# The place of three kinds of ScalarE copies, and of one product half, in a selective-scan kernel

## The reference, cut to what matters

```
xc    = causal 4-tap convolution of (in_proj_w @ ctx)      per channel
u     = silu(xc + conv_b)
B, C, dt = x_proj_w @ u                                     16, 16 and 32 rows
delta = softplus(dt_proj_w @ dt + dt_proj_b)
state = state * exp(delta * A) + (delta * u) * B            over 1024 positions, for 16 indices n
y     = (sum over n of state * C + D * u) * silu(layernorm(x) transposed)
x     = x + y transposed
xn    = layernorm(x)
out   = x + xn @ W_base.T + b_base + (two of eight rank-8 experts, gated by a softmax of the top two logits)
```

## Time and profile before

| | us |
|---|---|
| median of three runs | 2049.84 (2047.81 to 2057.35) |
| the profiled execution's own time | 2057.73 |
| its span, first to last instruction | 2055.7 |
| DVE busy | 1789.9 |
| POOL busy | 1729.5 |
| PE busy | 1767.3 |
| ACT busy | 1260.2 |
| mean granted TensorE clock | 0.916 of full speed |

### The profile page before, as it was taken

How to read it: one execution, slowest core, us unless ns; L and a number is a source line. 1 busy time by engine, 2 the same in 40 slices (tenths; PEclk the granted TensorE clock), 3 DMA queues, 4 the chain that set the end, 5 groups by cost and what they waited for, 6 DMA issues and landing times.

```text
span 2055.7 us, 23677 instructions
## 1 busy us (share of the span) xinstructions
PE 1767.3 (86%) x7996; PEld 1083.9 (53%) x7996; DVE 1789.9 (87%) x1435; ACT 1260.2 (61%) x1704; POOL 1729.5 (84%) x772
## 2 busy tenths in 40 slices
PE   9777777777788889898998889898888888888999
PEld 4344444454455555555555555555555555554554
DVE  3699999999999999999999999998999999996111
ACT  3466666656666676666666776666666676673331
POOL 0399999999999989899999999999999999996200
PEclk9887787777789999999999999999999999999999
DMA  4658665687766666688766666687676666666200
GB/s 157 243 190 290 202 205 194 194 297 269 229 214 201 222 205 216 214 301 279 244 207 220 222 212 211 224 283 260 225 223 214 203 213 216 220 205 217 80 31 31
DMA packets 158984, 435.87 MB, mean 212 GB/s; under 512 B 14640, under 2 KB 47664, under 8 KB 158864
## 3 DMA queue, kind: packets, MB, share of 16 engines
q1 hardware_dynamic: 155408, 421.78, 60.3%
q0 software_dynamic: 3456, 12.58, 3.1%
HBM read 383.46 MB, written 50.86 MB: 211 GB/s over the span
## 4 chain that ended last, share of the span: by engine, by line
DVE 40%; PE 31%; issue 19%; ACT 4%; POOL 3%; DMA 1%; DVEq 0%; SPq 0%; POOLq 0%; ACTq 0%
DVE state L1123 21%; DVE row L1108 13%; PE bank_a L544 9%; PE y_ps L488 6%; DVE conv L1100 3%; PE bank_b L544 3%; PE row L566 2%; POOL prod L1264 2%; PE row L482 2%; PE bank_b L439 1%; ACT decay L840 1%; PE bank_a L555 1%; DVE yy L1130 1%; PE bank_b L448 1%; PE bank_b L458 1%
## 5 line engine op out<-in xcount | busy, mean ns | idle before, releaser
L1264 POOL TENSOR_TENSOR prod<-state,c_rows 128x1024 f32<-128x1024 f32 x512 | 1207.2, 2383 | 87.9 <-DVE state L1123 47.6
L1123 DVE TENSOR_TENSOR_SCAN state<-decay,row 128x1024 f32<-128x1024 f32 x334 | 763.2, 2285 | 8.1
L488 PEld LDWEIGHTS y_ps<-ident,prod 128*128 128x128 f32 x4096 | 512.9, 151 | 274.9 <-issue 189.8
L488 PE MATMUL y_ps<-ident,prod 128*128 128x128 f32 x4096 | 581.8, 291 | 31.8 <-POOL prod L1264 31.4
L1108 DVE TENSOR_TENSOR row<-du,row 128x1024 f32<-128x1024 f32 x334 | 404.3, 1211 | 36.6 <-PE row L482 36.2
L1257 POOL TENSOR_TENSOR drive_rows<-du,b_rows 128x1024 f32<-128x1024 f32 x178 | 424.3, 2384 | 5.5 <-DMA b_rows<-bc_d 5.5
L544 PE MATMUL bank_a<-w_o,xnT 128*128 128x512 f32 x816 | 395.2, 615 | 19.6 <-DVE x L1170 19.6
L840 ACT ACTIVATE row<-delta,a 128x1024 f32<-128x1024 f32 x178 | 199.0, 1118 | 346.7 <-DVE state L1123 346.1
L1123 DVE TENSOR_TENSOR_SCAN state<-row,drive_rows 128x1024 f32<-128x1024 f32 x178 | 405.0, 2275 | 5.5 <-POOL drive_rows L1257 4.8
L840 ACT ACTIVATE decay<-delta,a 128x1024 f32<-128x1024 f32 x334 | 374.2, 1135 | 0.1
L482 PE MATMUL row<-parts,sel 96*128 96x512 bf16 x668 | 223.7, 420 | 157.3 <-DVE state L1123 151.1
(11 more groups left out here) (138 smaller groups left out, 1595.3 us busy)
## 6 DMA issues: line engine op xcount, KB each, us to landing
c_rows<-bc_d SPq DMA_DIRECT2D x512, 512.0 KB, 4.5
xrow<-in_x SPq DMA_DIRECT2D x32, 512.0 KB, 5.1
skip<-u_d SPq DMA_DIRECT2D x32, 512.0 KB, 9.0
yy_d<-yy SPq DMA_DIRECT2D x32, 512.0 KB, 6.5
b_rows<-bc_d SPq DMA_DIRECT2D x24, 512.0 KB, 9.4
u_d<-conv SPq DMA_DIRECT2D x24, 512.0 KB, 5.4
ctx<-u_d SPq DMA_DIRECT2D x48, 256.0 KB, 6.6
x<-in_x SPq DMA_DIRECT2D x24, 512.0 KB, 5.6
```

What stands on the lines that cost most here:

```text
L488: last = nc.tensor.matmul(y_ps[:, i * P:(i + 1) * P], source[:, i * P:(i + 1) * P], ident[:, :], start=(first and i % (H // P) == 0), stop ...
L1123: nc.vector.tensor_tensor_scan(state[:, q % STATES, :], factor, term, 0.0, ALU.mult, ALU.add).then_inc(scan_done, 1)
L1264: nc.gpsimd.tensor_tensor(prod[:, q % PRODS, :], state[:, q % STATES, :], c_rows[:, q % RING, :], ALU.mult).then_inc(prod_ready, 1)
```

## The change

On ScalarE, outside the last blocks, `take_v` in sections 1 and 2 and `take_gate` in sections 3 and 4 go from behind the section's decays to ahead of them. `take_turned`, of sections 3 and 4, stays where it is, so it is now behind `take_gate` and behind the decays. In section 11 `take_gates` goes ahead of `gate_rows`, behind the same table load. On TensorE, in the last blocks that are dense (15 and 23), the first product half stands in sections 8, 9, 10 and 11 in place of 6, 7, 9 and 10.

```diff
@@ tensor, section @@
                 if dense:
-                    if m in (6, 7, 9, 10):
-                        k = 2 * (6, 7, 9, 10).index(m)
+                    at = (8, 9, 10, 11) if last else (6, 7, 9, 10)
+                    if m in at:
+                        k = 2 * at.index(m)
                         product(j, 0, [k, k + 1], beside, True)
@@ scalar, section @@
+                last = r == NE - 1 and b + 1 < B
+                if not last and m in (1, 2) and E + 1 < NBLK:
+                    take_v(E + 1, m - 1)
+                if not last and m in (3, 4):
+                    take_gate(E, m - 3)
 
                 if (E, m + 1) in P_INDEX:
                     make_decay(E, m + 1)
...
-                last = r == NE - 1 and b + 1 < B
-                if not last and m in (1, 2) and E + 1 < NBLK:
-                    take_v(E + 1, m - 1)
...
                 if dense and m in (3, 4):
                     take_turned(j, m - 3, beside, True)
-                if not last and m in (3, 4):
-                    take_gate(E, m - 3)
...
                     if m == 11:
                         table(SILU)
-                        gate_rows(E + 1)
                 if dense and m == 11:
                     take_gates(j, beside)
+                if E + 1 < NBLK and m == 11:
+                    gate_rows(E + 1)
```

## The result

| | before | after |
|---|---|---|
| median, us (same chip) | 2053.6 (2047.81 to 2061.97) | 2086.22 (2082.67 to 2090.64) |
| ratio to before, 95% interval | | 1.0157 [1.0112, 1.0201] |
| span of the profiled execution | 2055.7 | 2088.6 |
| mean granted TensorE clock | 0.916 | 0.908 |

The change makes the kernel 32.6 us slower (23 to 41 by the interval). The forecast was 2059, the range 2038 to 2070: wrong, the time lies above the range. The direction and the mechanism were named; the size was over three times as large (+32.6 for +9.5). A small part is the start: the forecast was added to a median of 2049.8, and the median of this table is 2053.6.

The account below looks back on a forecast made before the run. VectorE was taken to set the pace, GpSimd just behind, with VectorE's waits mostly for TensorE. The terms +12 + 4 - 4 - 2.5 = +9.5 us on a median of 2049.8 gave 2059.3 us, range 2038 to 2070.

Parts of the forecast that it names:

- The order on ScalarE: Sections 3 and 4: ScalarE passes no waiting instruction, so xn's second turning starts 1.06 us later, 3.4 us after scan 2.
- The formula: Section 7's `spread` ends 10.14 us after the second turning starts, plus half the low-clock stretch behind that start.
- +12 for the projecting blocks: Sections 2 to 7, blocks 9 to 13 and 16 to 21: later second turning and low stretches cost +12 us (-1 to +24).
- D: Rival: nearly all blocks fall to the low clock, and late; two thirds of +24, in sum +18, 2068 us; chance 0.13.
- +4 for 14, 22 and 24 to 31: Blocks without projections, section 5: spare time shrinks from 1.63 to 0.57 us; low stretches cost +4 us (0 to 11).
- -4 for section 15: Sections 11 to 15, blocks without projections: turned gates copied 1.15 us earlier; half of 7.9 us waits goes, -4 (0 to -8).
- -2.5 for block 23, 0 for block 15: Moved product half and earlier gates' copy shorten VectorE's waits; GpSimd limits gains to -2.5 us (block 23), 0 (block 15).
- The non-dense blocks at 0: Blocks 0 to 8: they turn no xn, so the gate's copy delays nothing TensorE waits for; 0 us (-1 to 1).
- Rivals A to C: A: clock stays full, 2038, chance 0.22; B: low stretches keep places, 2048, 0.10; C: GpSimd absorbs gains, 2050, 0.05.
- A: Rival, sections 2 and 3: TensorE's 2.5 us idle is cut in pieces, clock stays full; -11.5 us, 2038; chance 0.22.

Follow-up runs that it names:

- gate_only: The kernel before with only `take_gate` moved ahead of its section's decays: 2079.63 us, ratio 1.0110 to before.
- after_turned_first: The changed kernel with `take_turned` put between `take_gate` and the decay: 2059.18 us, ratio 1.0021 to before.
- after_filled: The changed kernel with TensorE repeating transposes in idle time (first xn turning 4 times, gate's second turning twice): 2059.91 us, ratio 1.0028 to before.
- swapped_mid_filled: swapped_gates with the gates' transpose issued 8 times, the spread for section 12 twice, for section 13 three times: 2039.65 us, ratio 0.9931 to before.
- turned_swap: The kernel before with `take_turned` ahead of the decays and TensorE's second xn turning ahead of the gate's second: 2063.07 us, ratio 1.0034 to before.
- swapped_gates: The changed kernel, but `take_gate` where it was, `take_turned` ahead of the decay, xn's second turning ahead of the gate's: 2045.8 us, ratio 0.9963 to before.

## Why the prediction was wrong, point by point

**The order on ScalarE: right.** The second turning was put at 3.4 us after scan 2 and is at 3.38 in all 21 blocks that turn both; the 2.51 us wait is gone. ScalarE passes nothing that waits, as the Trainium skill ("PSUM — Partial Sum Buffer", section "Engine vs sequencer instructions") says. The trace agrees: in block 11 gate_only moves the turning from 2.35 to 3.38 us, and after_turned_first moves it back to 2.35, each by just the decay.

**The formula: right.** In block 12 the second turning starts 3.38 after scan 2 and the low stretch ends at 9.18: 3.38 + 10.14 + (9.18 - 3.38)/2 = 16.42; `spread` of section 7 ends at 788.40, 16.39 after. It comes out within 0.1 us in all eleven projecting blocks, before and after. What was wrong is what was put into it.

**+12 for the projecting blocks: this step failed.** Their waits in sections 5 and 7 rose from 7.9 to 30.8 us and the blocks from 643.5 to 665.0 us: +21.5. (The 7.6 us of the prediction left out 0.35 us in section 5 of block 20.) Its terms were a low stretch that ends at 6.3 on average, in eight blocks, and a chance of 0.4 in 11, 16 and 19. Ten of eleven fell; nine of them for 6.8 us, and the ends lie at 7.0 to 9.3, 8.6 on average. The average of 4.8 was carried 1.5 us later, as if the stretch were a thing that idle time carries with it. But the idle time now lies in three pieces (2.29, 1.20, 0.86 us) in front of work that used to run through, and the clock fell there in blocks that had never shown it. after_filled shows that this idle time matters: filled with repeats, it leaves no low stretch longer than 3.4 us there from block 10 on. The prediction had this case, D, at 13%, with +24, and priced it at two thirds.

**+4 for 14, 22 and 24 to 31: too small.** Section 5 costs 8.5 us (1.3 before) and section 8 2.8 (0): +10. A low stretch on the way was priced at 1.1 us, in four blocks of ten. It came in 22 and 25 to 31: in 22, 25 and 31, where it is 6.8 us long, section 5 waits 2.0 us, in the others 0.4 to 0.5. VectorE, after, block 25:

```profile
1549.43 1.23 DVE L1110 TENSOR_TENSOR row<-du,row 128x1024 f32<-128x1024 f32 x1 [2.00 <-PE row L482]
```

**-4 for section 15: half of it.** In the blocks without projections 7.9 became 6.1 us. (In the projecting blocks, put at 0, 4.5 became 1.4.) The early copy takes 1.12 us off the wait for the gates in block 25, and the idle time goes to the second product half, whose wait is for VectorE, as the text said:

```profile
1573.36 1.12 PE L555 MATMUL bank_a<-w_bdt,gT 65*128 65x512 f32 x2 [0.40 <-ACT gT L905]
...
1577.51 1.98 PE L544 MATMUL bank_a<-w_o,xnT 128*128 128x512 f32 x4 [2.15 <-DVE x L1172]
```

The five waits of 1.1 to 1.8 us became nine of 0.6 to 0.7: the waits were shortened and spread, not removed. In swapped_mid_filled, which fills that idle time, they are gone from these blocks.

**-2.5 for block 23, 0 for block 15: no gain.** The two blocks took 115.7 us and take 115.5. VectorE, after, block 23 and the start of block 16:

```profile
1457.61 2.29 DVE L1125 TENSOR_TENSOR_SCAN state<-row,drive_rows 128x1024 f32<-128x1024 f32 x1 [1.11 <-POOL drive_rows L1259]
...
1466.20 0.69 DVE L1172 TENSOR_TENSOR x<-x,bank_a 128x512 f32<-128x512 f32 x1 [1.73 <-PE bank_a L555]
...
1001.80 2.29 DVE L1125 TENSOR_TENSOR_SCAN state<-row,drive_rows 128x1024 f32<-128x1024 f32 x1 [1.67 <-POOL drive_rows L1259]
```

2.87 became 1.73 (in block 15 0.81), where no wait over 1 us was expected, and section 9's 0.72 went. But GpSimd's bound was read off one place, the start of block 24, and it holds at section 11 as well, where the scan waits 1.11 us for a drive. The wait at block 16 was foretold; that it would be 1.67 us was not.

**The non-dense blocks at 0: right within their spread,** 494.4 us in place of 492.9. In turned_swap, whose code for these blocks is that of before, they take 496.2.

The four sums, measured from the lengths of the blocks, are +21.5 (for +12), +9.3 (for +4 and -4), -0.2 (for -2.5) and +1.5 (for 0): 32.1 us, and the span grew by 32.9. Rivals A to C did not happen; the idle time did come back cut in pieces, as A said, and the clock fell all the same. What decides which block falls was not found: block 19 has the same delay and stays at the full clock.

## What to carry to other kernels

A copy that has to wait for a third engine belongs behind the copies and the work that are ready: in a queue that passes nothing, its wait is charged to each instruction behind it. Price the idle time of the matrix engine by where it will stand, not by where the low clock stands now, and when blocks get the same pattern of idle time, count on the low stretch in nearly all of them (ten of eleven here), not on an independent chance for each. When idle time there can't be removed, filling it with repeated work is a cheap test, and here, in swapped_mid_filled, also a gain.

## What was not expected of the hardware

- 300 more matmuls (x5867 for x5567), put into TensorE's idle time, made the kernel 6 us faster (swapped_mid_filled against swapped_gates). The granted clock over a whole execution lay between 0.922 and 0.929 in swapped_gates and between 0.934 and 0.937 in swapped_mid_filled.
- The low stretches may lock the pace. In after they start at 713.0, 774.4 and 835.8, and again at 1009.9, 1071.4 and 1132.8, 61.4 us apart each time; from scan 2 to scan 2 blocks 11, 12, 16 and 17 take 61.3 to 61.6 us, against 57.7, 60.1, 57.7 and 58.4 before. In blocks 26 to 30 both come every 54.6 us. It looks as if a block is lengthened until it meets the low stretch at the same place again, which would explain why nearly all blocks fell alike. That is argued from one trace; no run tested it.
- Executions of one kernel differ by more than most of these edits are worth. Before and turned_swap take 1300.2 and 1300.9 us from block 9 to 31, at a mean clock of 0.95 in both; the profiled executions differ by 5.4 us, and over 4 of them lie ahead of block 9, where the code is the same. The 0.34% between the two kernels is in the medians and not in these traces.
